# A two-lane decoder on one core: part of the second self attention's preparation moves from VectorE to GpSimd and ScalarE, with a new hand-written order

## The chip, the cores and the metric

The kernel is one launch on one core of a Trainium2 chip. The metric is device time in microseconds (us). The engines are TensorE (PE, matmuls; PEld is its weight load), VectorE (DVE), ScalarE (ACT), GpSimd (POOL) and SyncE (SP, which issues the DMAs). Each runs its own instruction stream in order and waits for others only by semaphores.

## The reference, cut to what matters

Two decoder layers on `x` of shape 4 x 256 x 128, six stages one after another, each added to `x`:

```python
x = x + _L0_attn_ref(_layernorm(x), ...)          # l0a: self attention, 16 heads, relative bias
x = x + _L0_xattn_ref(_layernorm(x), ctx, ctx)    # l0x: cross attention, 16 heads of 64
x = x + _L0_ffn_ref(_layernorm(x), ...)           # ffn: quantized, depthwise convolution, silu
x = x + _L1_attn_ref(_layernorm(x), ...)          # l1a: self attention (below)
x = x + _L1_xattn_ref(_layernorm(x), ctx, ctx)    # l1x: attention over heads within a token
x = x + _L1_ffn_ref(_layernorm(x), ...)           # moe: 8 experts, top 2, and a shared one
```

The stage that the change edits:

```python
def _L1_attn_ref(x, Wq, Wk, Wv, Wp, bp):          # H = 16, DQ = 4, HEAD_OUT = 8, keys and values shared by tiling
    q = x @ Wq
    k = jnp.tile(x @ Wk, (1, 1, G))
    v = jnp.tile(x @ Wv, (1, 1, G))
    ...
    scores = jnp.einsum('bhqd,bhkd->bhqk', q, k)
    scores = jnp.where(causal, -jnp.inf, scores)
    scores = (scores + _alibi_bias(t, scores.dtype)) / jnp.sqrt(jnp.asarray(DQ, scores.dtype))
    w = jax.nn.softmax(scores, axis=-1)
    ctx = jnp.einsum('bhqk,bhkd->bqhd', w, v).reshape(b, t, D_OUT)
    return ctx @ Wp + bp
```

## The kernel before

The four batches are cut into two lanes, A and B, of two batches each (512 tokens, held as 4 tiles of 128 tokens). Each lane runs the six stages in turn, in its own SBUF area and its own four PSUM banks; tile names begin with the lane and the stage (`A_l1a_qT`). Both lanes share the engines, so one lane's matmuls can run while the other lane is in a stretch of short dependent steps. A lane's stage begins when that lane's `x` of the stage before is updated.

What stands in which place in an engine's stream is decided by hand-written tables. Each stage has one generator per engine (`tensor`, `vector`, `scalar`, `gpsimd`, `sync`) which yields between pieces of work. `merged` (behind `TURNS`) steps through the generators of lane A, lane B, the weight levels (W) and late loads (L) in the order that a string such as `A4 B2 A2 W1` gives: four pieces of A, two of B, and so on. The yielded numbers only order pieces within one lane and stage; the engines' streams of the two lanes are mixed by `TURNS` alone. The numbers in the table are not times.

In l1a (`alibi_attention`, L1281) a projection of a token tile lands in PSUM as 80 query and key columns and 32 value columns, in float32. The scores are taken in bfloat16 from three parts of each number, high, middle and low:

- DVE (`split`, L1459 on) rounds the 80 columns to the high part (L1466), subtracts it (L1469, the rest), rounds the rest to the middle part (L1472) and subtracts that to get the low part (L1475). The link semaphore keeps each step behind the one before.
- POOL copies the queries' parts into a stack of 32 rows per head (L1392); ACT copies the values out of PSUM (L1406) and the keys' parts into the stack (L1410).
- PE transposes the stack in five groups (L1602), four of queries and one of keys, into two banks in turn. Group g waits for the copy of group g - 2.
- DVE copies the five groups from PSUM: four copies to `qT` (L1506, 128x512 bf16) and four of 32 rows to `kT` (L1510). `kT` and `vals` are set to zero before, by DVE (L1496, L1497), and the ones column of `vals` is set by DVE too (L1487).
- POOL's first work in the stage is the normalization's `rstd` (L160), which needs the variance that DVE wrote (L156), and on which DVE's four `xn` instructions wait (L165).

Beside this, l1a computes the keys and values of the later stage l1x from the context, which is known long before: 16 products per lane (L1561, L1566), biased by DVE (L1456) and ACT (L1401). They are the matmuls that can run while the preparation runs.

The cross attention of the first layer is l0x, with 32 head units per lane (16 heads, two batches). In a unit PE makes scores (L993, L995), DVE takes the maximum (L922), ACT the exponentials (L842), POOL the scaling by the sums (L825), PE three transposes (L1007), ACT the eviction (L859), PE the value products (L1020) and DVE an eviction for two units (L936). At the end comes the output product (L1028). In ffn, the silu (L1129) needs another activation table than the exponential (L842, L379).

## Time and profile before

| | before |
|---|---|
| median of 3 runs | 604.96 us (604.09 to 607.64) |
| profiled execution, whole time | 606.53 us |
| its span, first to last instruction | 604.6 us |
| PE busy | 522.7 us (86%) |
| DVE busy | 427.1 us (71%) |
| ACT busy | 330.7 us (55%) |
| POOL busy | 191.4 us (32%) |
| mean granted PE clock | 0.950 of full speed |

Shares of the chain that ended last: PE 64%, DVE 19%, ACT 5%, issue 5%, POOL 3%, DMA 2%. A stage's place in the span is read from the first and last start of its instructions: lane A runs ffn from about 244 to 292 us and l1a from there to 420; lane B runs ffn from 300 to 335 us and l1a from there to 432. The share of an engine over the whole span says little here, since the stages load the engines differently. The stretches by windows say more.

### The profile page before, as it was taken

The numbers are of one execution on the slowest core, as the hardware profiler recorded it, in microseconds if no ns is written. First come the engines' busy times: TensorE is split into PE (matmuls) and PEld (weight loads), VectorE is DVE, ScalarE is ACT, GpSimd is POOL, SyncE is SP. The second block draws the span as 40 slices with busy tenths as digits, with TensorE's granted clock in tenths as the row PEclk, the third lists the DMA queues.
The fourth block names the chain that finished last, engine by engine and source line by source line (L and its number), as shares of the span: only waits on it lengthen the run. The fifth ranks groups of instructions, "written<-read, shape, count | busy, mean of one in ns | idle before, by whom it ended". The sixth has DMA issues, their size and how long they took to land.

```text
span 604.6 us, 13037 instructions
## 1 busy us (share of the span) xinstructions
PE 522.7 (86%) x4832; PEld 323.9 (54%) x4842; DVE 427.1 (71%) x1261; ACT 330.7 (55%) x819; POOL 191.4 (32%) x288
## 2 busy tenths in 40 slices
...
GB/s 291 285 3 3 2 2 4 1 2 1 1 140 1 1 2 2 1 2 1 1 277 128 106 129 87 36 3 4 1 1 3 3 3 1 125 16 141 0 2 35
DMA packets 25890, 27.93 MB, mean 46 GB/s; under 512 B 18250, under 2 KB 22867, under 8 KB 24931
## 3 DMA queue, kind: packets, MB, share of 16 engines
...
## 4 chain that ended last, share of the span: by engine, by line
PE 64%; DVE 19%; ACT 5%; issue 5%; POOL 3%; DMA 2%; SPq 1%; POOLq 0%; DVEq 0%; ACTq 0%; another core or an unknown queue 0%
PE A_banks L312 4%; PE B_banks L312 4%; PE A_banks L2098 3%; PE B_banks L2098 3%; PE A_banks L1020 2%; PE A_banks L1007 2%; DVE A_l0a_nmax L340 2%; PE B_banks L1007 2%; PE B_banks L1823 2%; PE B_banks L1020 2%; PE B_banks L248 1%; PE B_banks L975 1%; PE A_banks L975 1%; PE B_banks L962 1%; PE B_banks L960 1%
## 5 line engine op out<-in xcount | busy, mean ns | idle before, releaser
L825 POOL TENSOR_TENSOR B_l0x_prob<-B_l0x_prob,B_l0x_inverted_sums 128x256 f32<-128x256 f32 (+1 forms) x32 | 26.0, 834 | 43.6 <-DVE B_l0x_inverted_sums L940 43.6
L825 POOL TENSOR_TENSOR A_l0x_prob<-A_l0x_prob,A_l0x_inverted_sums 128x256 f32<-128x256 f32 (+1 forms) x32 | 25.9, 829 | 39.3 <-DVE A_l0x_inverted_sums L940 39.2
L379 ACT ACTIVATE A_l0a_expT<-A_banks 128x512 f32<-128x512 f32 x32 | 18.6, 608 | 29.5 <-PE A_banks L327 29.5
L2098 PE MATMUL A_banks<-A_moe_xT,w_moe_rows 128*128 128x512 f32 x72 | 34.5, 597 | 0.1
L2098 PE MATMUL B_banks<-B_moe_xT,w_moe_rows 128*128 128x512 f32 x72 | 34.0, 595 | 0.0
L340 DVE TENSOR_REDUCE A_l0a_nmax<-A_banks 128x2 f32<-128x512 f32 x32 | 21.8, 689 | 14.6 <-PE A_banks L248 14.1
L842 ACT ACTIVATE A_l0x_prob<-A_l0x_prob,A_l0x_nmax 128x128 f32<-128x128 f32 x64 | 28.2, 447 | 2.5 <-DVE A_l0x_nmax L922 2.5
L842 ACT ACTIVATE B_l0x_prob<-B_l0x_prob,B_l0x_nmax 128x128 f32<-128x128 f32 x64 | 28.2, 446 | 0.9 <-DVE B_l0x_nmax L922 0.9
L340 DVE TENSOR_REDUCE B_l0a_nmax<-B_banks 128x2 f32<-128x512 f32 x32 | 21.8, 687 | 9.0 <-PE B_banks L248 8.6
L160 POOL TENSOR_TENSOR A_l0a_rstd<-A_l0a_ve,w_const_rows 128x4 f32<-128x4 f32 x2 | 2.0, 1012 | 79.9 <-DVE A_l0a_ve L156 79.9
L379 ACT ACTIVATE A_l1a_expT<-A_banks 128x384 f32<-128x384 f32 x32 | 15.3, 494 | 20.1 <-PE A_banks L292 20.1
L859 ACT ACTIVATE B_l0x_probT<-B_banks 128x384 f32<-128x384 f32 x32 | 15.5, 483 | 18.6 <-PE B_banks L1007 18.6
L379 ACT ACTIVATE B_l0a_expT<-B_banks 128x512 f32<-128x512 f32 x32 | 18.5, 606 | 10.2 <-PE B_banks L327 10.2
L1994 ACT ACTIVATE B_moe_h<-B_banks,w_moe_rest_rows 128x512 f32<-128x512 f32 x18 | 12.3, 686 | 20.8 <-PE B_banks L2098 20.6
L1007 PE MATMUL B_banks<-w_const_rows,B_l0x_prob 128*128 128x128 f32 x96 | 17.7, 295 | 6.4 <-ACT B_l0x_probT L859 4.1
L1994 ACT ACTIVATE A_moe_h<-A_banks,w_moe_rest_rows 128x512 f32<-128x512 f32 x18 | 12.3, 684 | 18.5 <-PE A_banks L2098 18.5
L859 ACT ACTIVATE A_l0x_probT<-A_banks 128x384 f32<-128x384 f32 x32 | 15.5, 484 | 10.9 <-PE A_banks L1007 10.8
L922 DVE CUSTOM_DVE_ANT_0 A_l0x_prob<-A_banks,A_l0x_mask_q 128x128 f32<-128x128 f32 x64 | 18.9, 351 | 3.4 <-PE A_banks L995 3.3
L379 ACT ACTIVATE B_l1a_expT<-B_banks 128x384 f32<-128x384 f32 x32 | 15.3, 492 | 10.0 <-PE B_banks L292 9.9
L340 DVE TENSOR_REDUCE B_l1a_nmax<-B_banks 128x2 f32<-128x512 f32 (+1 forms) x24 | 16.3, 687 | 6.0 <-PE B_banks L256 5.6
L340 DVE TENSOR_REDUCE A_l1a_nmax<-A_banks 128x2 f32<-128x512 f32 (+1 forms) x24 | 16.3, 689 | 5.9 <-PE A_banks L256 5.6
L922 DVE CUSTOM_DVE_ANT_0 B_l0x_prob<-B_banks,B_l0x_mask_q 128x128 f32<-128x128 f32 x64 | 18.9, 349 | 1.4 <-PE B_banks L995 1.4
...
## 6 DMA issues: line engine op xcount, KB each, us to landing
...
```

What stands on the lines that cost most here:

```text
L312: ins = pe.matmul(bank[r:r + self.rows, second:S], lhsT, rhs, start=(part == 0), stop=(part == parts - 1), skip_group_check=True)
L340: dve.tensor_reduce(out, scores, AX, ALU.max, negate=True).then_inc(self.s_mx.sem, 1)
L379: act.activation(self.expT[:, u % self.ring, :], self.exp_bank(u)[:, 0:self.W], ACT.Exp, scale=self.scale).then_inc(self.s_p.sem, 1)
L825: ins = pool.tensor_tensor(pair, pair, bcast(rz[:, g % 2, i, :], 2, n), ALU.mult)
L842: ins = act.activation(part, part, ACT.Exp, bias=nmax[:, b, i, h:h + 1], scale=-1.0, accum_out=zsum[:, g % 2, i, u % 2:u % 2 + 1])
L859: act.activation(probT[:, u % 4, :], bank[2][:, 0:W], ACT.Copy).then_inc(s_pt.sem, 1)
L922: ins = dve.tensor_tensor_reduce(prob[:, (2 * p + j) % RING, at:at + n], bank[j][:, at:at + n], mask_q[:, b, at:at + n], 1.0, 3e38, ALU.ad ...
L975: pe.matmul(q_bank(c)[:, :], w["l0x_q"][:, c * P:(c + 1) * P], xT[:], start=True, stop=True).then_inc(s_q.sem, 1)
L1007: ins = pe.transpose(bank[2][:, c * P:(c + 1) * P], prob[:, u % RING, c * P:(c + 1) * P], w["ident"][:])
L1020: ins = pe.matmul(bank[3][HD * j:HD * (j + 1), part * P:S], vals[:, b * SB + part, h * HD:(h + 1) * HD], pT[:, S:W] if part else pT[:, 0:S ...
L1994: act.activation(h1[:, n % 2, :], hidden_bank(2 * n)[:, :], ACT.Identity, bias=w["moe_b1"][:, e, part:part + 1]).then_inc(s_h1.sem, 1)
L2098: pe.matmul(hidden_bank(k)[:, :], w["moe_w3" if which else "moe_w1"][:, ORDER[i], part, :], xT[:], start=True, stop=True).then_inc(s_h.sem, 1)
```

## The change

Four edits in l1a and one in the tables:

- The middle rounding and the low difference of the split are POOL's (2 instructions per tile, 4 tiles, per lane). DVE signals the rest (`s_rest`), POOL signals the middle part (`s_mid`) and then the low one (`s_split`).
- ACT's copy of the values waits for `s_rest` and no longer for `s_split`, and the keys' copies are a piece of their own.
- The four copies of the queries' transposed parts are ACT's. The keys' ones stay with DVE, with a semaphore of their own (`s_qT`, `s_kT` in place of `s_qkT`).
- `kT` and `vals` are zeroed by POOL at the start of its stage, and the ones column is set by POOL behind `rstd`.
- `TURNS` has new strings for all five engines, so the two lanes are mixed in another way from l0a to moe.

```diff
@@ gpsimd
+        yield 0.5
+        pool.memset(kT[:], 0.0).then_inc(s_kz.sem, 1)
+        pool.memset(vals[:], 0.0).then_inc(s_kz.sem, 1)
         yield 1.5
         w.loaded(pool, "l1a")
         norm.gpsimd_rstd(pool)
         yield 1.6
         yield 2.0
+        pool.wait_ge(*s_kz(2))
+        pool.memset(vals[:, :, :, DV:DV + 1], 1.0).then_inc(s_init.sem, 1)
...
         for t in range(TT):
-            yield 9.0 + 3.5 * t
+            yield 8.5 + 3.5 * t
+            pool.wait_ge(*s_rest(t + 1))
+            mid, lo, rest = sp_[:, t % 2, 1, :], sp_[:, t % 2, 2, :], sr[:, t % 2, :]
+            pool.tensor_copy(mid, rest).then_inc(s_mid.sem, 1)
+            yield
+            pool.wait_ge(*s_mid(t + 1))
+            pool.tensor_tensor(lo, rest, mid, ALU.subtract).then_inc(s_split.sem, 1)
+            yield
             pool.wait_ge(*s_split(t + 1))
@@ scalar, values(t)
+            act.wait_ge(*s_rest(t + 1))
+            act.activation(vals[:, t, :, 0:DV], ...).then_inc(s_v.sem, 1)
+            yield 9.5 + 3.5 * t
             act.wait_ge(*s_split(t + 1))
-            act.activation(vals[:, t, :, 0:DV], ...).then_inc(s_v.sem, 1)
...
         yield from interleaved([all_keys(), all_values()])
+        for g in range(4):
+            yield 22.0 + g
+            act.wait_ge(*s_stT(g + 1))
+            act.activation(qT[:, g, :], stack_bank(g).bitcast(BF16), ACT.Copy).then_inc(s_qT.sem, 1)
@@ vector, split
-            link.add(dve.tensor_tensor(sr[:, t % 2, :], qk, hi, ALU.subtract))
-            yield due
-            link.wait()
-            link.add(dve.tensor_copy(mid, sr[:, t % 2, :]))
-            yield due
-            link.wait()
-            dve.tensor_tensor(lo, sr[:, t % 2, :], mid, ALU.subtract).then_inc(s_split.sem, 1)
+            dve.tensor_tensor(sr[:, t % 2, :], qk, hi, ALU.subtract).then_inc(s_rest.sem, 1)
@@ vector
-        dve.memset(kT[:], 0.0).then_inc(s_kz.sem, 1)
-        dve.memset(vals[:], 0.0).then_inc(s_kz.sem, 1)
         yield from interleaved([all_values(), all_splits()])
-        for g in range(5):
...
+        yield 26.0
+        dve.wait_ge(*s_kz(2))
+        dve.wait_ge(*s_stT(5))
+        for j in range(HK):
+            r = slice(SW * j, SW * (j + 1))
+            ins = dve.tensor_copy(kT[r, j, :], stack_bank(4).bitcast(BF16)[r, :])
+        ins.then_inc(s_kT.sem, 1)
@@ TURNS (all five strings are new; the first line of one)
-        "A4 B2 A2 B2 A5 B2 A3 B3 A4 B2 A1 B3 A10 B3 A3 B1 A1 B1 ...
+        "A4 B2 A2 B2 A5 B2 A3 B3 A1 B2 A2 B1 A2 B1 A3 B1 A7 B9 ...
```

Three places of the new order follow. The first is ACT's stream around lane A's silu. L842 is the exponential of lane B's cross attention, L859 its eviction, L1136 and L1129 lane A's convolution and silu. Before:

```order
L842 ACTIVATE B_l0x_prob,B_l0x_zsum<-B_l0x_prob,B_l0x_nmax 128x256
L859 ACTIVATE B_l0x_probT<-B_banks 128x384
L1129 ACT_TABLE_LOAD
L1129 ACTIVATE A_ffn_conv<-A_ffn_conv 128x512 x4
L859 ACTIVATE B_l0x_probT<-B_banks 128x384
L842 ACT_TABLE_LOAD
L842 ACTIVATE B_l0x_prob,B_l0x_zsum<-B_l0x_prob,B_l0x_nmax 128x128
L842 ACTIVATE B_l0x_prob,B_l0x_zsum<-B_l0x_prob,B_l0x_nmax 128x256
```

Now:

```order
L859 ACTIVATE B_l0x_probT<-B_banks 128x384
L1136 ACTIVATE A_ffn_conv<-A_ffn_h,w_ffn_rows 128x512 x2
L1129 ACT_TABLE_LOAD
L1129 ACTIVATE A_ffn_conv<-A_ffn_conv 128x512 x4
L1143 ACTIVATE A_ffn_r<-A_banks,A_ffn_scale 128x512 x4
L1146 ACTIVATE A_ffn_q2T<-A_banks 128x1024
L1124 ACTIVATE B_ffn_rowinv<-B_banks 128x512
```

All of lane B's exponentials now stand ahead of lane A's silu, so the table is not loaded back for them, and it is still the right one at lane B's silu. Before, there are three loads from here to the end of lane B's silu, now there is one; the load before the exponentials of l1a (L379) stands in both.

The second place is PE's stream from lane A's sums over the hidden columns (L1253) through its transposes (L1262) and down product (L1269). L1007, L993, L995, L1020 and L1028 are lane B's cross attention. Before:

```order
L1253 MATMUL A_banks<-w_const_rows,A_ffn_conv 128x128 x16
L1007 MATMUL B_banks<-w_const_rows,B_l0x_prob 128x128 x3
L993 MATMUL B_banks<-B_l0x_kT,B_l0x_qT 128x128 x2
L995 MATMUL B_banks<-B_l0x_kT,B_l0x_qT 128x256 x2
L1007 MATMUL B_banks<-w_const_rows,B_l0x_prob 128x128 x3
L1020 MATMUL B_banks<-B_l0x_probT,B_l0x_vals 64x256 x2
L1020 MATMUL B_banks<-B_l0x_probT,B_l0x_vals 64x128 x2
```

Now (L1235 is the first product of lane B's ffn, L1563 lane A's context values):

```order
L1028 MATMUL B_banks<-w_l0x_vo_rows,B_l0x_qT 128x128 x16
L1253 MATMUL A_banks<-w_const_rows,A_ffn_conv 128x128 x16
L1262 MATMUL A_banks<-w_ident_bf,A_ffn_q_114 128x128 x16
L1269 MATMUL A_banks<-w_ffn_q,A_ffn_q2T 128x128 x16
L1235 MATMUL B_banks<-B_ffn_diag,w_const_rows 128x128 x4
L1563 MATMUL A_banks<-w_l1x_rows,A_ctxT 128x512
L1240 MATMUL B_banks<-w_ident_bf,B_ffn_xq 128x128 x4
```

Lane B's cross attention is now over, with its output product, ahead of lane A's sums. Behind lane A's own output product (its last L1028) 19 units of lane B had their transposes left before, and 9 have now. At the first row of lane B in l1a, the streams of both kernels stand at the same piece in both lanes again.

The third place is POOL's stream where lane B enters l1a. Before:

```order
L1392 COPY A_l1a_expT<-A_l1a_split 128x16x4 x2
L160 TENSOR_TENSOR B_l1a_rstd<-B_l1a_ve,w_const_rows 128x4
L1375 TENSOR_TENSOR B_l1a_row_bias<-w_l1a_rows 128x32
L1376 MEMSET B_l1a_expT 128x80x2
L1378 TENSOR_TENSOR B_l1a_row_bias<-B_l1a_row_bias,w_l1a_rows 128x32
```

Now:

```order
L1405 COPY A_l1a_expT<-A_l1a_split 128x16x4 x2
L1371 MEMSET B_l1a_kT 128x2048
L1372 MEMSET B_l1a_vals 128x512
L160 TENSOR_TENSOR B_l1a_rstd<-B_l1a_ve,w_const_rows 128x4
L1379 MEMSET B_l1a_vals 128x16
L1381 TENSOR_TENSOR B_l1a_row_bias<-w_l1a_rows 128x32
```

The two memsets stand between the start of the stage and `rstd`, and the larger has 2048 elements per partition, where DVE's had 1024 (of four bytes each).

## Rows read from the trace of the kernel before

**Rows 1.** Windows; us, busy us of each engine (x instructions), clock, DMA share, GB/s

```profile
core 0: us, PE busy (x) PEld busy (x) DVE busy (x) ACT busy (x) POOL busy (x), PEclk, DMA share, GB/s
...
244.30:345.80 101.50, 77.51 (x528) 49.45 (x529) 84.32 (x268) 58.27 (x154) 32.16 (x74) 0.90 0.25 75
345.80:604.60 258.80, 233.43 (x2626) 161.08 (x2632) 190.28 (x442) 127.82 (x244) 73.05 (x76) 0.98 0.11 35
```

**Rows 2.** The same view, lane B's ffn beside lane A's l1a

```profile
292.00:335.00 43.00, 34.12 (x219) 20.85 (x217) 36.41 (x107) 23.16 (x54) 11.59 (x37) 0.92 0.49 148
```

**Rows 3.** The chain that ended last, 333 to 341 us: start, us, what

```profile
333.91 1.13 DVE B_x L1229 x4
335.03 0.33 DVE A_l1a_qT L1506
...
337.75 0.30 DVE A_l1a_qT L1506
...
339.59 0.91 DVE B_l1a_kT L1496
...
340.56 0.48 DVE B_l1a_vals L1497
```

**Rows 4.** Instructions of one line; xcount: duration in ns min/median/max, first and last start

```profile
L1472 DVE CAST A_l1a_split<-A_l1a_rest_qk x4: 191/198/201, 307.8 to 331.9; 128x80 bf16<-128x80 f32 x4
...
L1475 DVE TENSOR_TENSOR A_l1a_split<-A_l1a_rest_qk,A_l1a_split x4: 232/234/243, 310.1 to 332.8; 128x80 bf16<-128x80 f32 x4
...
L1506 DVE COPY A_l1a_qT<-A_banks x4: 414/416/425, 334.9 to 337.7; 128x512 bf16<-128x512 bf16 x4
```

**Rows 5.** Instructions of one line, as in rows 4, for POOL

```profile
L497 POOL CAST A_l0a_split<-A_l0a_rest_qk x4: 396/400/400, 17.3 to 29.5; 128x256 bf16<-128x256 f32 x4
...
L500 POOL TENSOR_TENSOR A_l0a_split<-A_l0a_rest_qk,A_l0a_split x4: 667/668/678, 17.8 to 30.0; 128x256 bf16<-128x256 f32 x4
...
L1379 POOL MEMSET A_l1a_parts<- x1: 522/522/522, 297.1 to 297.1; 128x512 bf16 x1
```

**Rows 6.** Instructions of one line, for an ACT copy of 512 columns

```profile
L1423 ACT ACTIVATE A_l1a_xT<-A_banks x1: 598/598/598, 303.8 to 303.8; 128x512 f32<-128x512 f32 x1
```

**Rows 7.** Timeline: start, us, engine, line, instruction, idle before it and its releaser

```profile
336.93 1.01 POOL L160 TENSOR_TENSOR B_l1a_rstd<-B_l1a_ve,w_const_rows 128x4 f32<-128x4 f32 x1 [2.97 <-DVE B_l1a_ve L156]
```

**Rows 8.** Timeline of ACT around lane A's silu, 272 to 278 us

```profile
272.27 1.28 ACT L1129 ACT_TABLE_LOAD   x1
...
273.57 2.19 ACT L1129 ACTIVATE A_ffn_conv<-A_ffn_conv 128x512 f32<-128x512 f32 x4
...
276.15 1.28 ACT L842 ACT_TABLE_LOAD   x1
```

**Rows 9.** Groups, 244.3 to 345.8 us: xcount | busy us, mean ns | idle before, releaser

```profile
L859 ACT ACTIVATE B_l0x_probT<-B_banks 128x384 f32<-128x384 f32 x19 | 9.2, 483 | 12.6 <-PE B_banks L1007 12.6
...
L922 DVE CUSTOM_DVE_ANT_0 B_l0x_prob<-B_banks,B_l0x_mask_q 128x128 f32<-128x128 f32 (+1 forms) x28 | 8.3, 349 | 0.5 <-PE B_banks L995 0.5
...
L936 DVE COPY B_l0x_qT<-B_banks 128x256 f32<-128x256 f32 x11 | 4.6, 420 | 4.7 <-PE B_banks L1020 4.7
...
L922 DVE DVE_READ_ACCUMULATOR2_ANT B_l0x_nmax<- 128x1 f32 x28 | 2.2, 80 | 0.0
...
L940 DVE RECIPROCAL B_l0x_inverted_sums<-B_l0x_zsum 128x4 f32<-128x4 f32 x8 | 1.4, 172 | 0.8 <-ACT B_l0x_prob L842 0.7
```

**Rows 10.** Groups of PE, 190 to 240 us, lane B's units

```profile
L1007 PE MATMUL B_banks<-w_const_rows,B_l0x_prob 128*128 128x128 f32 x39 | 6.9, 285 | 1.0 <-DVE B_l0x_qT L875 0.9
...
L995 PE MATMUL B_banks<-B_l0x_kT,B_l0x_qT 64*128 64x256 f32 x30 | 4.6, 377 | 0.0
L1020 PE MATMUL B_banks<-B_l0x_probT,B_l0x_vals 128*64 128x256 f32 (+1 forms) x40 | 4.3, 336 | 0.0
L993 PE MATMUL B_banks<-B_l0x_kT,B_l0x_qT 64*128 64x128 f32 x32 | 3.9, 322 | 0.0
```

**Rows 11.** Instructions of one line: lane A's xn in l1a, 128x128

```profile
L165 DVE TENSOR_SCALAR A_l1a_xn<-A_x,A_l1a_mv,A_l1a_rstd x4: 327/530/882, 296.6 to 297.7; 128x128 f32<-128x128 f32 x4
```

More of the change, by code:

```diff
@@ L1404, in values @@
         def values(t):
+            act.wait_ge(*s_rest(t + 1))
+            act.activation(vals[:, t, :, 0:DV], bank[2 + t % 2][:, NQK:W].rearrange("p (h d) -> p h d", h=HK), ACT.Copy).then_inc(s_v.sem, 1)
+            yield 9.5 + 3.5 * t
             act.wait_ge(*s_split(t + 1))
-            act.activation(vals[:, t, :, 0:DV], bank[2 + t % 2][:, NQK:W].rearrange("p (h d) -> p h d", h=HK), ACT.Copy).then_inc(s_v.sem, 1)
             for part, i, n in split_columns(K_PARTS):
@@ L1427, in all_values @@
                     act.wait_ge(*s_init(2))
-                values(t)
+                yield from values(t)
         yield from interleaved([all_keys(), all_values()])
+        for g in range(4):
+            yield 22.0 + g
+            act.wait_ge(*s_stT(g + 1))
+            act.activation(qT[:, g, :], stack_bank(g).bitcast(BF16), ACT.Copy).then_inc(s_qT.sem, 1)
         for n in range(U + 8):
@@ L1464, in split @@
             qk = bank[2 + t % 2][:, 0:NQK]
-            hi, mid, lo = (sp_[:, t % 2, i, :] for i in range(3))
+            hi = sp_[:, t % 2, 0, :]
             link.add(dve.tensor_copy(hi, qk))
@@ L1484, in all_splits @@
         def all_splits():
-            yield 3.0
-            dve.wait_ge(*s_kz(2))
-            dve.memset(vals[:, :, :, DV:DV + 1], 1.0).then_inc(s_init.sem, 1)
             for t in range(TT):
```

27 lines of the change are left out of this document (9 added, 18 removed), and 46 rows, old and new, of the table TURNS.

## The prediction

> **What bounds the kernel now.** I read the windows first, since a share over the whole span mixes six stages in two lanes. I cut the span at two events: the end of lane A's output product of the cross attention, at 244.3 us, and lane A's first masked score product, at 345.8 us. Between them lie both feed-forward stages and the preparation that the change edits. There PE is busy 77.5 of 101.5 us at a mean clock of 0.90, while DVE is busy 84.3 us; behind 345.8 us PE is busy 233.4 of 258.8 us at 0.98 [rows 1]. So most of PE's idle time to be had by this change lies in the middle stretch, and DVE is the busiest engine in it. With lane B's feed-forward beside lane A's preparation DVE has 36.4 of 43.0 us, a share of 0.847 [rows 2]. The chain of waits was read next, for what of the edited work lies on the path. It goes through DVE with three copies of the queries' parts of lane A and then both memsets of lane B [rows 3]. PE, and everything of lane B behind it, waits there.
>
> **The edit, DVE's side.** Per lane go 4 middle roundings of 0.198 us, 4 low differences of 0.234 us and 4 copies of 0.416 us [rows 4], which is 3.39 us, and memsets of 0.91 and 0.48 us [rows 3], together 4.8 us; the ones memset is too small to count. In the middle stretch this is all of lane A's and the memsets of lane B, 4.8 + 1.4 = 6.2 us. On the chain itself I find 0.91 + 0.48 for lane B's memsets and about 1.0 us for three copies, of which the first and the last stand with 0.33 and 0.30 us [rows 3], so 2.4 us. That is the least that leaves; the most is the whole of 6.2 us.
>
> **The edit, what it adds.** POOL gets a middle rounding and a low difference per tile. The same pair in the first self attention takes 0.396 and 0.668 us at 256 columns [rows 5]; at 80 columns I bound it by those from above and by 80/256 of them from below (0.12 and 0.21), and take 0.26 and 0.35. Behind them on POOL stand the queries' stack copies and behind these PE's transposes. Only the last tile of a lane can be late by it, by some 0.3 us, and in lane A that is covered by lane B's tail. The keys' parts on ACT wait as long, but the values no longer wait for the low part. ACT's copies of the queries' parts: a copy of 512 float32 columns takes 0.598 us there [rows 6] against 0.416 on DVE, so 0.18 us more for each of four. The groups alternate between two banks and no longer queue behind lane B's statistics on DVE, so I take nothing for lane A; without that cover it is 0.7 us per lane.
>
> The memsets in front of `rstd` are a real price. POOL's memset of 512 bf16 elements takes 0.522 us [rows 5]. At that rate 2048 elements take 2.1 us; the least is DVE's 0.91 us [rows 3]. With `vals`, 0.5 us, POOL is busy 2.6 us from the start of the stage. In lane B the stage starts at 335.04 us, when `x` is done [rows 3], and `rstd` starts at 336.93 us [rows 7], 1.9 us later. So `rstd` is late by 0.7 us (nothing if the memset is as quick as DVE's), and with it `xn`, on which the chain stands. Lane A has feed-forward work of lane B to do on DVE meanwhile. I take +0.7 us.
>
> **The new order.** It changes three things that I can price.
>
> First, two table loads go. Lane A's silu stays behind its load at 272.27 us; the reload for lane B's exponentials, 1.28 us at 276.15 us [rows 8], goes, and so does the load of lane B's silu, which is off the chain. Between 0 and 2.6 us; it is part of the stretch below and is not counted twice. ACT starts its first silu at 273.57 us, at once behind the load that took 1.28 us from 272.27 us [rows 8]. The Trainium skill (ScalarE: Activation LUTs, section What ACT_TABLE_LOAD costs) says that a switch costs a drain of about 1.38 us besides its 1.283 us. The load agrees with the row, and the drain does not show in it; by the page two switches would be worth 5.3 us, by the row 2.6 us.
>
> Second, lane B is further on when lane A leaves the cross attention. 19 of its evictions stood in the middle stretch [rows 9], and 9 stand there now by the order. So 10 units move ahead. Their work on PE per unit, from lane B's groups between 190 and 240 us, is 6.9/13 + 4.6/15 + 4.3/10 + 3.9/16 = 1.51 us [rows 10] (the counts divided by 3, 2, 4 and 2 instructions per unit). PE is the bound ahead of the cut, so the first stretch grows by 10 x 1.51 = 15.1 us. Their work on DVE is 8.3/14 + 2.2/14 + 4.6/22 + 1.4/16 = 1.05 us per unit [rows 9] (two L922 and two accumulator reads per unit, one L936 and one L940 per two units).
>
> Third, with 10 units and the edit gone, DVE has 84.3 - 6.2 - 10.5 = 67.6 us of work in the middle stretch. At the share of 0.847 [rows 2] it takes 67.6 / 0.847 = 79.8 us. If DVE never paused it would take 67.6 us, and at the share of the stretch before, 84.3 / 101.5 [rows 1], 81.4 us. I take 79.8, since rows 2 is already the mixture of lane B's feed-forward with lane A's preparation that the new stretch mostly is. So the middle shrinks by 101.5 - 79.8 = 21.7 us, and 15.1 us of that is given back ahead of it: 6.6 us remain.
>
> Against this stands that PE now has nothing of lane B between lane A's hidden sums and its down product. PE's clock in the stretch is 0.90 already [rows 1], and a further pause may drop it to the lower of its two levels (1.2 of 2.4 GHz) for the matmuls that follow. I take +1 us, between 0 and 5. Behind the second cut both orders stand at the same piece when lane B enters the second self attention, and the work behind it is the same; I take 0, within 3 us either way, for an order of which no row shows the effect.
>
> **Sum.** -6.6 + 0.7 + 1.0 = -4.9 us. On the profiled execution (606.53 us, its span 604.6 us) this gives 601.6 us. The median of the runs is 604.96 us, 1.6 us below it, so the forecast is 604.96 - 4.9 = 600.0 us, rounded.
>
> **The rivals.**
>
> *POOL's new work holds DVE up.* The four xn instructions of lane A, of one shape, took 0.327 us at the quickest and 0.882 at the slowest [rows 11], and POOL was busy then. If each of lane A's and lane B's 8 new instructions stops DVE for its own length, this costs 8 x (0.26 + 0.35) = 4.9 us, and the forecast goes back to 604.9 us: no change. For it speaks the spread of rows 11; against it, that the instructions are short and DVE would have to be at one of the hindered forms each time. The Trainium skill states such a rule (SBUF — State Buffer, section Who interferes with whom): GpSimd and VectorE share one pair of ports, taken whole for an instruction, and copies, casts and tensor_scalar of VectorE can need it. The spread of rows 11 agrees.
>
> *The new mixture is worth nothing, and only the edit's part on the chain counts.* This is the case if the units moved ahead cost there what they free later. Then it is -2.4 + 0.7 = -1.7 us, 603.3 us: no change too. For it speaks that the work of every engine is the same in total; against it, that 10 units cost PE 15.1 us and the DVE-bound stretch more.
>
> *PE stands uncovered between the two feed-forward stages, and it is slower.* Lane A's chain from the hidden sums to `x` has had lane B's heads beside it, and now lane B's own feed-forward begins only at its end. If the two stages then follow each other rather than overlap, the middle stretch is twice the 35 us that lane B's stage takes (300 to 335 us) plus the 11 us from there to 345.8 us, and 9 units of 1.51 us before, 94.6 us. With 15.1 us given back ahead, 0.7 us for `rstd` and 2 us of lower clock it is 94.6 - 101.5 + 15.1 + 2.7 = +10.9 us, 615.9 us; halfway there, 608 us. It decides from a middle stretch of 84.7 us on (101.5 - 15.1 - 1.7). For it speaks the order of PE's stream; against it, that on DVE lane B's statistics already stand among lane A's last steps.
>
> **How the numbers follow.** The forecast has 0.50, of which some 0.08 is a stretch nearer to DVE never pausing (67.6 us, which would give 588 us). The port rival has 0.13, the neutral mixture 0.13, the uncovered PE 0.24. A change within 0.5% (3 us) can't be told from none, so faster is below 601.9 us and slower above 608.0 us. The forecast lies 1.9 us below the first bound, and some of its cases fall short of it (0.06), while a few of the rivals' come out faster: faster 0.48, same 0.29, slower 0.23. The range is 591 to 611 us: half of the way to an unpaused DVE on one side, and most of the way to the third rival on the other. The forecast's own range is 595 to 604 us.
>
> **What would show it.** In the profile after: the time from the end of lane A's last L1028 to its first masked score near 80 us, against 101.5; the first of these near 259 us, against 244.3; two table loads fewer; DVE's busy time in l1a less by 4.8 us per lane; POOL's memset of `kT` near 2.1 us and lane B's `rstd` 2.6 us behind its `x`; the xn and copies of DVE no slower than 0.88 us beside POOL. It would be wrong if the first cut moved by much more than 15 us, if the middle stretch stayed above 85 us, or if a difference of over 3 us arose behind the second cut.

## The result, and the profile after

The changed kernel takes 588.07 us (median of 4 runs, 586.74 to 589.35) against 604.93 us before (4 runs, 604.09 to 607.64): a ratio of 0.972, 95% interval 0.968 to 0.976, so 16.9 us faster. Forecast were 600.0 us and a range of 591 to 611. Two further sets of runs gave 588.28 us (0.971, 0.968 to 0.975) and 589.0 us (0.974, 0.970 to 0.978). The profiled execution has a span of 587.6 us, 17.0 less than the one that the prediction read.

The windows of the changed kernel, cut at the events of [rows 1] and also where lane A's l0x begins (126.0 us) and where its l1x begins (408.7 us). Columns as in [rows 1].

```profile
0.00:126.00 126.00, 100.53 (x1010) 50.72 (x1011) 85.46 (x232) 66.00 (x151) 34.21 (x69) 0.91 0.20 71
126.00:253.50 127.50, 123.05 (x816) 73.47 (x815) 81.23 (x379) 91.88 (x321) 60.33 (x79) 1.00 0.05 18
253.50:330.10 76.60, 58.45 (x386) 35.69 (x386) 66.99 (x192) 44.55 (x106) 30.97 (x78) 0.89 0.28 91
330.10:408.70 78.60, 73.81 (x891) 53.89 (x890) 52.67 (x147) 45.28 (x116) 5.88 (x24) 0.98 0.22 60
408.70:587.50 178.80, 159.96 (x1740) 108.03 (x1744) 136.81 (x284) 83.56 (x132) 71.14 (x60) 0.98 0.08 28
```

The first cut comes at 253.5 us, 9.2 later than before; the middle stretch has 76.6 us against 101.5, 24.9 less; what follows has 257.5 against 258.8, 1.3 less [rows 1]. The sum is -17.0 us. The same view of the kernel before, for the two halves of its first stretch (lane A's l0x begins at 124.9 us) and the two parts behind the middle:

```profile
0.00:124.90 124.90, 96.69 (x891) 48.40 (x892) 83.43 (x223) 60.41 (x139) 34.04 (x69) 0.88 0.20 72
124.90:244.30 119.40, 115.11 (x793) 65.00 (x793) 69.05 (x329) 84.16 (x282) 52.15 (x69) 1.00 0.05 19
345.80:421.00 75.20, 68.38 (x839) 50.20 (x838) 54.89 (x156) 40.16 (x105) 3.69 (x17) 1.00 0.20 54
421.00:604.60 183.60, 165.05 (x1790) 110.87 (x1796) 135.39 (x287) 87.66 (x139) 69.36 (x60) 0.97 0.08 27
```

Compare row by row. In the second half PE is busy 96% of the time in both kernels, and the new order's extra work there, 7.9 us of PE, costs 8.1 us. In the first half 119 more matmuls run (1010 against 891), and the stretch grows by 1.1 us only. PE had paused there for 28.2 of 124.9 us, at a mean clock of 0.88. Now it pauses for 25.5 us, at 0.91, and its busy time is only 3.8 us higher.

Lane B's head units that are left for the middle stretch, to be held against [rows 9] (19 evictions, 28 maxima, 11 copies):

```profile
L859 ACT ACTIVATE B_l0x_probT<-B_banks 128x384 f32<-128x384 f32 x9 | 4.3, 483 | 6.7 <-PE B_banks L1007 6.7
L936 DVE COPY B_l0x_qT<-B_banks 128x256 f32<-128x256 f32 x6 | 2.5, 420 | 0.5 <-PE B_banks L1020 0.4
```

The new instructions of POOL and ACT in lane B's l1a (count, ns min/median/max, starts):

```profile
L1371 POOL MEMSET B_l1a_kT<- x1: 1805/1805/1805, 322.1 to 322.1; 128x2048 bf16 x1
L1396 POOL CAST B_l1a_split<-B_l1a_rest_qk x4: 249/254/254, 334.1 to 345.8; 128x80 bf16<-128x80 f32 x4
L1399 POOL TENSOR_TENSOR B_l1a_split<-B_l1a_rest_qk,B_l1a_split x4: 336/337/338, 334.5 to 346.1; 128x80 bf16<-128x80 f32 x4
L1449 ACT ACTIVATE B_l1a_qT<-B_banks x4: 592/594/597, 349.2 to 352.4; 128x512 bf16<-128x512 bf16 x4
```

And two places of its timeline, where such a memset meets DVE (start, us, instruction, idle before it):

```profile
291.85 1.80 POOL L1371 MEMSET A_l1a_kT<- 128x2048 bf16 x1 [1.36 <-DVE A_x L1229]
292.62 1.78 DVE L1182 TENSOR_SCALAR B_ffn_r<-B_ffn_r 128x512 f32<-128x512 f32 x1
293.59 0.52 POOL L1372 MEMSET A_l1a_vals<- 128x512 f32 x1
...
322.11 1.80 POOL L1371 MEMSET B_l1a_kT<- 128x2048 bf16 x1 [0.24 <-DVE B_x L1229]
...
323.41 0.99 DVE L156 TENSOR_SCALAR B_l1a_ve<-B_l1a_mv 128x4 f32<-128x4 f32 x1
...
323.85 0.52 POOL L1372 MEMSET B_l1a_vals<- 128x512 f32 x1
...
324.55 1.02 POOL L160 TENSOR_TENSOR B_l1a_rstd<-B_l1a_ve,w_const_rows 128x4 f32<-128x4 f32 x1 [0.17 <-DVE B_l1a_ve L156]
```

Lane B's variance step takes 0.99 us (0.17 for lane A's), and the feed-forward's L1182 1.78 us (0.41 to 0.43 for lane A and in the kernel before). `rstd` starts 2.5 us behind `x`.

The forecast expected PE to pause in the middle stretch and to be slower behind it. These are the two rows of the changed kernel in which that happens (columns as in [rows 1]):

```profile
276.90:284.30 7.40, 2.44 (x19) 1.80 (x18) 6.92 (x26) 3.50 (x7) 1.11 (x3) 1.00 0.79 296
284.30:294.60 10.30, 7.78 (x42) 5.22 (x42) 9.69 (x30) 2.58 (x4) 3.74 (x6) 0.50 0.18 73
```

### The profile page after: what moved, and what is told of

The parts are those of the page before. It is cut to its first block, busy times and chain, and to the rows that moved or that the text cites. A ratio compares the mean times of both kernels' runs of the same rounds, so it can differ in the third digit from the quotient of the medians.

```text
span 587.6 us, 13037 instructions
## 1 busy us (share of the span) xinstructions
PE 515.8 (88%) x4832; PEld 321.8 (55%) x4842; DVE 423.2 (72%) x1231; ACT 331.3 (56%) x825; POOL 202.5 (34%) x310
## 4 chain that ended last, share of the span: by engine, by line
PE 65%; DVE 18%; ACT 4%; issue 4%; SPq 3%; POOL 3%; DMA 2%; POOLq 0%; DVEq 0%; ACTq 0%
PE A_banks L2101 5%; PE A_banks L312 4%; PE B_banks L312 4%; PE B_banks L2101 4%; DVE A_l0a_nmax L340 2%; PE A_banks L1007 2%; PE A_banks L1020 2%; DMA B_l1x_values<-B_l1a_v_tokens 2%; PE B_banks L1867 2%; SPq L276 1%; PE B_banks L1007 1%; DVE B_l0a_nmax L340 1%; PE B_banks L1028 1%; PE A_banks L1877 1%; SPq L1364 1%
## 5 line engine op out<-in xcount | busy, mean ns | idle before, releaser
L379 ACT ACTIVATE A_l0a_expT<-A_banks 128x512 f32<-128x512 f32 x32 | 18.3, 604 | 20.5 <-PE A_banks L327 20.5
L842 ACT ACTIVATE B_l0x_prob<-B_l0x_prob,B_l0x_nmax 128x128 f32<-128x128 f32 x64 | 28.2, 446 | 1.3 <-DVE B_l0x_nmax L922 1.3
L842 ACT ACTIVATE A_l0x_prob<-A_l0x_prob,A_l0x_nmax 128x128 f32<-128x128 f32 x64 | 28.2, 449 | 0.0
L379 ACT ACTIVATE B_l0a_expT<-B_banks 128x512 f32<-128x512 f32 x32 | 18.2, 601 | 15.0 <-PE B_banks L327 15.0
L859 ACT ACTIVATE A_l0x_probT<-A_banks 128x384 f32<-128x384 f32 x32 | 15.5, 484 | 15.6 <-PE A_banks L1007 15.6
L379 ACT ACTIVATE A_l1a_expT<-A_banks 128x384 f32<-128x384 f32 x32 | 15.1, 491 | 15.2 <-PE A_banks L292 15.0
L859 ACT ACTIVATE B_l0x_probT<-B_banks 128x384 f32<-128x384 f32 x32 | 15.4, 482 | 14.3 <-PE B_banks L1007 14.2
L379 ACT ACTIVATE B_l1a_expT<-B_banks 128x384 f32<-128x384 f32 x32 | 15.1, 493 | 11.8 <-PE B_banks L292 11.5
L1007 PE MATMUL B_banks<-w_const_rows,B_l0x_prob 128*128 128x128 f32 x96 | 17.2, 289 | 5.0 <-POOL B_l0x_prob L825 2.0
```

The costliest lines, as they stand in the source:

```text
L379: act.activation(self.expT[:, u % self.ring, :], self.exp_bank(u)[:, 0:self.W], ACT.Exp, scale=self.scale).then_inc(self.s_p.sem, 1)
L842: ins = act.activation(part, part, ACT.Exp, bias=nmax[:, b, i, h:h + 1], scale=-1.0, accum_out=zsum[:, g % 2, i, u % 2:u % 2 + 1])
L859: act.activation(probT[:, u % 4, :], bank[2][:, 0:W], ACT.Copy).then_inc(s_pt.sem, 1)
L1007: ins = pe.transpose(bank[2][:, c * P:(c + 1) * P], prob[:, u % RING, c * P:(c + 1) * P], w["ident"][:])
```

## The experiments

Ratios are to the kernel before, on the same chip, with 95% intervals. Where an order is made from two, the tables alone differ; of these the first PE line that differs is shown (A and B are the lanes, the number is how many pieces; e3 and e11 against the changed kernel, e4 and e10 against e2).

### Order or edit

**e1, e13: the order alone.** The code before, with the new tables. DVE's 24 displaced pieces of both lanes had to be placed; e1 puts them beside their neighbours, e13 by their time.

```diff
-"A4 B2 A2 B2 A5 B2 A3 B3 A4 B2 A1 B3 A10 B3 A3 B1 A1 B1 A2 B3 A1 B1 A1 B2 A1 B1 A1 B1 A1 B3 A6 B1 A2 B2 A1 B1 A3 B2 A2 B3 A3 B1 A1 B2 A1 B2 A5 B4 A3 B1 A1 "
+"A4 B2 A2 B2 A5 B2 A3 B3 A1 B2 A2 B1 A2 B1 A3 B1 A7 B9 A1 B1 A1 B3 A2 B1 A1 B2 A6 B2 A1 B3 A2 B1 A1 B5 A1 B1 A1 B1 A1 B1 A4 B1 A1 B1 A1 B2 A3 B1 A1 B1 A1 B2 "
```

> The kernel before with the changed kernel's order of pieces on every engine; the DVE instructions that the edit took away stay on DVE, right behind the piece they belong to, and lane B's copies of the queries' parts stand together. Theory 1 (the order carries most of it: the middle stretch, and in the first self attention the two lanes stand nearer in step, so that PE has more to do between 60 and 80 us and gets its full clock earlier; the edit is worth only its 4 to 5 us): 592 to 594 us, first cut near 253.5 us. Theory 2 (the edit alone makes the gain, the order is only its carrier): 604 to 606 us. Theory 3 (neither alone, they need each other, because the order was made for the lighter DVE): over 600 us here and over 600 us with the edit alone.

> As the order alone, but DVE's middle roundings, low differences and copies of the queries' parts stand in DVE's order at the time at which GpSimd and ScalarE do them in the changed kernel, one by one between the other lane's pieces. Theory 1 (the gap between the order alone and both is real, lane A's copies into kT and lane B's xn queue up on DVE): 594 to 597 us, as the first version at 596.1. Theory 2 (the gap is made by the bunched copies): 590 to 592 us.

Measured: 596.13 us, 0.9875 (0.9856 to 0.9894), and 593.03 us, 0.9813 (0.9790 to 0.9835). Both times lie nearest to the first theory of e1, e1's 2 us above its range, and e13's between its own two ranges. So the order alone is worth 11.3 us (9.9 to 12.7), two thirds of the result. The two placings of the displaced pieces are 3 us apart, so the placing matters as much as one of the edit's parts. Windows of e13: the first half, and the middle.

```profile
0.00:126.80 126.80, 101.54 (x1010) 51.05 (x1011) 85.35 (x231) 66.06 (x151) 34.30 (x69) 0.89 0.20 71
...
254.30:333.90 79.60, 58.29 (x385) 35.71 (x385) 70.70 (x210) 42.70 (x102) 23.79 (x64) 0.89 0.29 91
```

**e2, e14: the edit alone.** The changed code with the old tables, placed in the same two ways.

```diff
-"A4 B2 A2 B2 A5 B2 A3 B3 A1 B2 A2 B1 A2 B1 A3 B1 A7 B9 A1 B1 A1 B3 A2 B1 A1 B2 A6 B2 A1 B3 A2 B1 A1 B5 A1 B1 A1 B1 A1 B1 A4 B1 A1 B1 A1 B2 A3 B1 A1 B1 A1 B2 "
+"A4 B2 A2 B2 A5 B2 A3 B3 A4 B2 A1 B3 A10 B3 A3 B1 A1 B1 A2 B3 A1 B1 A1 B2 A1 B1 A1 B1 A1 B3 A6 B1 A2 B2 A1 B1 A3 B2 A2 B3 A3 B1 A1 B2 A1 B2 A5 B4 A3 B1 A1 "
```

> The changed kernel's code with the order of pieces of the kernel before (the new pieces of GpSimd and ScalarE stand where they come ready; one score product of lane A goes ahead of lane B's third group of stack transposes, without which the order locks). Theory 1: the edit is worth 4 to 5 us by what it takes off the chain in the second self attention, so 600 to 601 us, with the first cut unchanged at 244 us. Theory 2: 588 us. Theory 3: over 600 us, at or above the kernel before.

> As the edit alone, but GpSimd's and ScalarE's new pieces stand where their DVE forms began in the kernel before, and no product of lane A is moved ahead. Theory 1 (in the old order lane B's statistics and PE's queue, not the edited work, set lane B's time, so the edit brings nothing): 603 to 605 us. Theory 2 (the edit's gain was lost by the placing of ScalarE's copies): 599 to 601 us.

Measured: 604.64 us, 0.9997 (0.9978 to 1.0016), and 602.2 us, 0.9980 (0.9957 to 1.0003). e2 misses the 600 to 601 us of its first theory, and e14 lies between its two. In the old order the edit is worth 1.2 us, or nothing. In the new one it is worth the step from 0.9813 to 0.971 to 0.974, 4 to 6 us with some 3 us of uncertainty. The windows of e14 and e2 show where it would have come:

```profile
245.10:342.60 97.50, 74.61 (x529) 46.69 (x529) 78.94 (x250) 60.32 (x158) 38.93 (x88) 0.93 0.27 76
```

```profile
0.00:121.40 121.40, 95.04 (x891) 48.52 (x892) 82.71 (x222) 60.44 (x139) 34.51 (x69) 0.90 0.21 74
...
240.90:338.10 97.20, 74.09 (x527) 47.96 (x527) 79.44 (x250) 60.33 (x158) 38.75 (x88) 0.93 0.25 75
338.10:599.20 261.10, 233.95 (x2626) 161.36 (x2632) 187.13 (x430) 130.22 (x248) 75.44 (x84) 0.98 0.11 36
```

DVE pauses for 18.6 us in e14's middle, and for 17.2 in the kernel before [rows 1]; with the new order it is 8.9 us in e13 and 9.6 in the changed kernel. That less work on DVE buys little where it pauses anyway fits these figures, but no run tests it by itself.

**e9: the kernel before, profiled again.**

> The kernel before, profiled a second time, to see how much of a stretch's length is the clock of one execution. Theory 1 (the profiled execution that the prediction read had 30.7 us at the lower clock before its first cut, where the kernel with the edit alone, whose work is the same up to there, had 23.9 us and came to the cut at 240.6 us against 244.0): with 24 us at the lower clock the first cut is at 241 us here and the middle stretch 98 to 102 us. Theory 2 (the clock plays no part, the 3.4 us are the edit's): cut at 244 us whatever the clock.

```profile
0.00:127.50 127.50, 99.52 (x891) 50.23 (x892) 84.02 (x223) 60.53 (x139) 34.03 (x69) 0.85 0.19 70
127.50:246.90 119.40, 115.13 (x793) 65.00 (x793) 69.06 (x329) 84.15 (x282) 52.15 (x69) 1.00 0.05 19
246.90:347.10 100.20, 77.22 (x529) 49.10 (x529) 84.05 (x268) 58.32 (x154) 32.16 (x74) 0.90 0.25 76
```

The clock came out lower, not higher, so the expectation's case didn't occur. Its rule holds: with the same 891 matmuls in the first half, clocks of 0.85, 0.88 and 0.90 (e9, before, e2) go with 127.5, 124.9 and 121.4 us. One profile of the first half is good to 3 us, no better, so all of them are averaged here. The six with the old order have 121.4 to 127.5 us, 124.9 on average, and the thirteen with the new order 125.0 to 127.9, 126.4 on average: 1.5 us more. The second half has 119.4 or 119.5 us in every profile with the old order throughout, and 127.4 or 127.5 with the new one. The first cut comes at 244.3 us on average with the old order (four profiles) and at 253.8 us with the new one (twelve), 9.5 us later.

### Where the order's gain comes from

**e3: new order in the first half, old behind.**

```diff
-"A1 B1 A1 B1 A1 B1 A2 B3 A1 B1 A2 B1 A2 B1 A1 B1 A3 B1 A1 B1 A3 B1 A4 B1 A1 B1 A3 B1 A8 B4 A1 B2 A1 B1 A1 B2 A1 B2 A1 B1 A2 B2 A1 B1 A1 B1 A2 B1 A1 B3 A4 B1 "
+"A1 B1 A1 B1 A1 B1 A2 B3 A1 B1 A2 B1 A2 B1 A1 B1 A3 B1 A1 B1 A3 B1 A4 B1 A1 B1 A3 B1 A15 B4 A1 B1 A2 B1 A1 B1 A2 B1 A2 B1 A1 B1 A2 B1 A3 B1 A2 B1 A3 B1 A2 "
```

> The changed kernel's code; the new order up to the start of lane A's cross attention (about 124 us), the old order for all that is left. Theory 1: the first self attention keeps its better clock, and lane A leaves it no later than before although lane B is further on; behind it the old order has fewer pieces of lane B left to place. 595 to 599 us. Theory 1b (the first stage's order brings nothing, all comes behind 124 us): 601 to 606 us, since lane B's lead made there is bought with lane A's time and given away by the old order.

602.77 us, 0.9987 (0.9965 to 1.0009). The first half has 127.3 us, within the range of the new order; the second 115.1 us, 4.3 less than before, but the middle is 98.7 us. The first stage's order brings nothing by itself (theory 1b): the old order spends lane B's lead before the middle.

**e4: old order in the first half, new behind. e10: old order up to lane A's ffn, new behind.** The new order expects lane B further on; the missing pieces of B then run in one go, 19 on PE in e4, 32 in e10:

```diff
-"B2 A2 B2 A4 B1 A1 B1 A4 B2 A1 B2 A1 B1 A2 B3 A1 B1 A1 B2 A1 B4 A2 B1 A1 B7 A1 B1 A2 B1 A1 B1 A2 B1 A2 B1 A1 B1 A2 B1 A3 B1 A2 B1 A3 B1 A2 B1 A2 B1 A1 B1 A1 "
+"B2 A2 B2 A4 B1 A1 B1 A1 B19 A6 B4 A1 B2 A1 B1 A1 B2 A1 B2 A1 B1 A2 B2 A1 B1 A1 B1 A2 B1 A1 B3 A4 B1 A2 B2 A3 B2 A2 B1 A3 B2 A1 B1 A4 B4 A2 B1 A1 B2 A2 B1 "
...
-"B12 A2 B3 A1 B7 A1 B8 A1 B1 A1 B1 A2 B2 A1 B7 A11 B3 A4 B1 A5 B4 A1 B1 A8 B1 A12 B4 A2 B2 A2 B1 A2 B4 A2 B1 A2 B3 A3 B1 A2 B1 A1 B7 A2 B4 A1 B4 A1 B4 A1 B2 "
+"B32 A2 B1 A1 B8 A6 B1 A1 B1 A1 B1 A9 B1 A7 B4 A1 B1 A10 B2 A12 B3 A2 B2 A2 B1 A2 B4 A2 B1 A2 B3 A2 B1 A1 B3 A1 B1 A2 B16 A1 B4 A4 B3 A2 B1 A1 B2 A6 B2 A1 "
```

> The changed kernel's code; the old order up to the start of lane A's cross attention, the new order behind it. Theory 1: PE's clock before 100 us is as in the kernel before (23 us at its lower level without a break, and again at 77 and 84 us), and the rest is as in the changed kernel: 588 + 4 to 6 = 592 to 594 us. Theory 1b: 588 us, as the changed kernel, within 0.5%.

> The changed kernel's code; the old order up to lane A's first piece of the feed-forward stage, the new order behind it: lane B's 10 units that the new order has ahead of this point now stand behind it, all before lane A's feed-forward. Theory 1 (the 10 units cost PE their 13 us wherever they stand without cover, and what counts is that DVE has only 9 left beside the feed-forward stages): lane A's feed-forward begins 11 to 13 us behind the first cut of 241 to 244 us, then as the changed kernel: 588 to 591 us. Theory 2 (it counts that they lie beside lane A's heads, where they fill PE's pauses): 594 to 600 us.

598.89 us, 0.9913 (0.9884 to 0.9943), and 601.35 us, 0.9944 (0.9914 to 0.9974). Both miss theory 1, e4 also its theory 1b, and e10 lies 1.4 us above the range of its theory 2: built this way, lane B's lead costs most of what it is worth. Windows of e4 (the first half as before, the catching up, both of these together, from there to the first cut, the middle):

```profile
0.00:124.90 124.90, 96.77 (x886) 49.30 (x890) 83.41 (x222) 60.44 (x139) 34.06 (x69) 0.88 0.20 72
124.90:141.40 16.50, 12.77 (x114) 5.71 (x106) 2.57 (x11) 8.43 (x17) 0.00 (x0) 1.00 0.00 0
0.00:141.40 141.40, 109.54 (x992) 55.00 (x992) 85.98 (x232) 68.88 (x156) 34.06 (x69) 0.89 0.18 63
141.40:267.40 126.00, 120.79 (x833) 72.50 (x834) 81.18 (x379) 88.69 (x315) 60.34 (x79) 0.99 0.05 18
267.40:341.80 74.40, 56.99 (x386) 34.90 (x387) 66.37 (x192) 44.50 (x106) 31.27 (x78) 0.91 0.29 94
```

And e10's catching up, and its time from there to the second cut:

```profile
244.20:268.10 23.90, 18.86 (x156) 12.72 (x154) 13.02 (x58) 13.78 (x51) 8.16 (x10) 1.00 0.00 1
268.10:340.60 72.50, 54.92 (x372) 33.68 (x374) 65.92 (x193) 43.99 (x105) 31.41 (x78) 0.91 0.29 95
```

Not all of e4's 16.5 us is the price of catching up. Of the 114 matmuls 12 are lane A's products of the context, 5.9 us, which lane A needs anyway:

```profile
L962 PE MATMUL A_banks<-A_ctxT,w_l0x_rows 128*128 128x512 f32 x8 | 3.9, 605 | 0.0
L960 PE MATMUL A_banks<-w_l0x_vo_rows,A_ctxT 128*128 128x512 f32 x4 | 2.0, 619 | 0.0
```

The fair comparison is the time at which lane A can begin its feed-forward. e4 has run the same matmuls by then as the changed kernel, e10 12 more, and they get there at 267.4 us (e4), 268.1 (e10) and 253.5 (changed). Against the 244.3 us before, the lead costs 23 or 24 us where lane A stands still for it, and 9 us where it is mixed in. Of the 13.9 us between e4 and the changed kernel 7.2 are pauses of PE (37.1 against 29.9) and 6.7 are its busy time (230.3 against 223.6), for the same work. The busy time can be less by the clock (0.89 and 0.99 in e4's two windows, 0.91 and 1.00 in the changed kernel's) and by matmuls that follow more closely on each other; no run separates the two.

**e11: new order up to lane B's l1a, old behind.**

```diff
-"A1 B1 A1 B1 A2 B1 A2 B1 A3 B1 A1 B1 A1 B12 A2 B1 A1 B8 A6 B1 A1 B1 A1 B1 A9 B1 A7 B4 A1 B1 A10 B2 A12 B3 A2 B2 A2 B1 A2 B4 A2 B1 A2 B3 A2 B1 A1 B3 A1 B1 A2 "
+"A1 B1 A1 B1 A2 B1 A2 B1 A3 B1 A1 B1 A1 B12 A2 B1 A1 B8 A6 B1 A1 B1 A1 B1 A9 B1 A7 B4 A1 B1 A10 B1 A12 B4 A2 B2 A2 B1 A2 B4 A2 B1 A2 B3 A3 B1 A2 B1 A1 B7 A2 "
```

> The changed kernel's code; the new order up to lane B's second self attention (322 us), the old order behind it. Theory 1 (as predicted, the order behind that point is worth nothing, within 3 us): 587 to 591 us. Theory 2 (in the profiles the changed kernel needs 178.9 us from lane A's last cross attention to its end against 183.6 us, 4.7 us less, and the three kernels with the new order there all need 178 to 179 us): 591 to 594 us.

591.46 us, 0.9785 (0.9747 to 0.9824), 3 us above the changed kernel, with overlapping intervals and at the border between the two theories. In the profile the part behind the second cut has 260.4 us against 257.4, of which lane A's l1x and what follows is 181.9 against 178.8 us:

```profile
328.70:407.20 78.50, 69.81 (x840) 51.27 (x838) 52.26 (x145) 42.61 (x110) 6.17 (x25) 0.98 0.23 61
407.20:589.10 181.90, 163.52 (x1789) 110.36 (x1794) 135.22 (x287) 87.59 (x139) 69.33 (x60) 0.98 0.08 28
```

### The parts of the edit, in the new order

**e5** and **e17** are the changed kernel again.

> The changed kernel, timed once more beside its variants, so that each is compared on the same chip. 588 us, 587 to 590. Theory 1 (of the gap of 8 us between the order alone, 596.1 us, and both, all is real): the same ratio to the kernel before as in the first comparison, 0.972. Theory 2 (part of that gap is the difference between two sets of runs): 0.975 to 0.98.

> The changed kernel beside e16: 587 to 589 us, ratio to the kernel before 0.971 to 0.974.

Their figures stand at the head of this part. **e6, e7, e8** each give DVE one part back:

```diff
 # e6
-            pool.tensor_copy(mid, rest).then_inc(s_mid.sem, 1)
+            dve.tensor_copy(mid, rest).then_inc(s_mid.sem, 1)
...
-            pool.tensor_tensor(lo, rest, mid, ALU.subtract).then_inc(s_split.sem, 1)
+            dve.tensor_tensor(lo, rest, mid, ALU.subtract).then_inc(s_split.sem, 1)
 # e7
-            act.activation(qT[:, g, :], stack_bank(g).bitcast(BF16), ACT.Copy).then_inc(s_qT.sem, 1)
+            dve.tensor_copy(qT[:, g, :], stack_bank(g).bitcast(BF16)).then_inc(s_qT.sem, 1)
 # e8
-        pool.memset(kT[:], 0.0).then_inc(s_kz.sem, 1)
-        pool.memset(vals[:], 0.0).then_inc(s_kz.sem, 1)
+        dve.memset(kT[:], 0.0).then_inc(s_kz.sem, 1)
+        dve.memset(vals[:], 0.0).then_inc(s_kz.sem, 1)
```

> The changed kernel with the middle rounding and the low difference of the second self attention on DVE again, 16 instructions in pieces of their own, put into DVE's order at the time at which GpSimd had them. Theory 1 (the edit is worth DVE's time in the DVE-bound middle stretch): 8 x 0.198 + 8 x 0.234 = 3.5 us slower, less what GpSimd's slower pair (0.25 + 0.34 us) gave, so 2 to 3.5 us: 590 to 591.5 us. Theory 2 (only what stands on the chain counts, and these don't): within 1 us of the changed kernel.

> The changed kernel with the four copies of the queries' transposed parts of each lane on DVE again (0.416 us each against 0.6 us on ScalarE), put into DVE's order at the time at which ScalarE had them. Theory 1 (DVE's time in the middle stretch): 4 x 0.416 = 1.7 us slower for lane A's, and lane B's stand on the chain where either engine is waited for: 588 + 1 to 2.5 us. Theory 2 (copies on the chain are quicker on DVE): 0 to 1 us faster than the changed kernel.

> The changed kernel with the two memsets of each lane on DVE again, behind its xn; the ones stay with GpSimd. Theory 1: 2 x (0.91 + 0.48) = 2.8 us more on DVE in or at the end of the middle stretch, less the 0.6 us by which rstd is earlier: 2 us slower, 590 us. Theory 2 (the sets hide behind the wait for PE's first products): within 1 us.

Measured 589.15, 589.90 and 589.67 us, beside 588.28: +0.9, +1.6 and +1.4 us, ratios 0.9748, 0.9761 and 0.9753 with intervals of 0.003 either way. None is told from nothing alone, so these runs don't decide between the theories of any of the three. Together they make 3.9 us by the medians and 7 by the ratios (each against 0.9714), which agrees with the 4 to 6 us of the whole edit. No part makes it by itself.

**e15: two table loads put back.**

```diff
         act.activation(rowinv[:], bank[0][:, :], ACT.Copy).then_inc(s_ri.sem, 1)
+        if lane.name == "B":
+            act.activation(y[:, HC - 1, 0:1], w["ident"][:, 0:1], ACT.Exp)
```

> The changed kernel with one exponential of a single column put on ScalarE between the silus of the two lanes (in lane B's feed-forward stage, behind its row copy), which costs a load for it and another for lane B's silu: two table loads of 1.28 us more, as many as in the kernel before. Theory 1 (both stand on lane B's path, which sets when its second self attention starts): 588 + 2.6 = 590.6 us. Theory 2 (the chain through that stage is DVE's, ScalarE has time there): 588 to 588.5 us. By the Trainium skill (ScalarE: Activation LUTs, What ACT_TABLE_LOAD costs) a drain of about 1.38 us would come with each load; if it does and both are on the path, 593.3 us.

587.71 us, 0.9713 (0.9682 to 0.9745), against the 0.9714 of the changed kernel: nothing, theory 2. ACT's timeline there:

```profile
291.84 0.60 ACT L1124 ACTIVATE B_ffn_rowinv<-B_banks 128x512 f32<-128x512 f32 x1 [3.86 <-PE B_banks L1237]
292.45 1.28 ACT L1126 ACT_TABLE_LOAD   x1
293.75 0.20 ACT L1126 ACTIVATE B_ffn_conv<-w_const_rows 128x1 f32<-128x1 f32 x1
...
303.69 1.28 ACT L1131 ACT_TABLE_LOAD   x1
```

The load starts 0.01 us behind the copy's end, and the exponential 0.02 us behind the load's: no drain is seen here either.

**e12, e16: the memsets elsewhere on POOL**, behind `rstd` (e12) or behind the small copies (e16), the keys' as 1024 uint32.

```diff
-        pool.memset(kT[:], 0.0).then_inc(s_kz.sem, 1)
-        pool.memset(vals[:], 0.0).then_inc(s_kz.sem, 1)
...
         norm.gpsimd_rstd(pool)
+        pool.memset(vals[:], 0.0).then_inc(s_kz.sem, 1)
+        pool.memset(kT[:].bitcast(U32), 0).then_inc(s_kz.sem, 1)
```

> The changed kernel with GpSimd's two memsets of the second self attention behind its rstd, and that of the keys as 1024 uint32 elements instead of 2048 bf16. Theory 1: rstd of lane B starts 0.6 us earlier (1.9 us behind its x, as before the change), and this stands on the chain: 587.3 to 587.7 us, a gain of 0.6 us, which 5 rounds can hardly tell. The memset of 1024 uint32 takes 0.9 us if the time goes by elements, 1.8 us if by bytes. Theory 2 (the later sets delay the values' copies on ScalarE): 588.5 us or more.

> The changed kernel with GpSimd's memsets of the second self attention (values, then keys as 1024 uint32, then the ones) behind its small copies, 2.3 us after rstd, when xn is done. Theory 1 (the memsets hold DVE's tensor_scalar instructions up): lane B's variance step takes 0.17 us and its xn 1.1 to 1.3 us, rstd starts 1.7 us behind x, and of that 0.8 to 1.4 us reach the end: 586.8 to 587.4 us if the changed kernel is at 588.2. Theory 2 (lane B's preparation waits for PE anyway): no difference that 5 rounds can tell.

589.71 us, 0.976 (0.9723 to 0.9798), and 589.34 us, 0.9754 (0.9728 to 0.978), beside e17's 589.0. By their times both miss theory 1 and agree with theory 2; what theory 1 says of the place itself happens in part. The first two rows are e12's, the other two e16's:

```profile
L1375 POOL MEMSET B_l1a_kT<- x1: 953/953/953, 326.4 to 326.4; 128x1024 uint32 x1
L165 DVE TENSOR_SCALAR B_l1a_xn<-B_x,B_l1a_mv,B_l1a_rstd x4: 336/900/1412, 326.0 to 327.8; 128x128 f32<-128x128 f32 x4
```

```profile
L156 DVE TENSOR_SCALAR B_l1a_ve<-B_l1a_mv x1: 170/170/170, 322.9 to 322.9; 128x4 f32<-128x4 f32 x1
L165 DVE TENSOR_SCALAR B_l1a_xn<-B_x,B_l1a_mv,B_l1a_rstd x4: 329/534/886, 324.3 to 325.4; 128x128 f32<-128x128 f32 x4
```

In both `rstd` starts 1.7 us behind `x`, 0.8 earlier than in the changed kernel. In e12 an xn instruction then takes up to 1.41 us (0.75 at most in the changed kernel), and the gain is gone. In e16 the variance step is not held up, and an xn takes up to 0.89 us. From the start of lane B's l1a to its first score product it has 31.1 us (321.6 to 352.7) against 31.5 (322.1 to 353.6), which no comparison of these runs can tell. No version here is faster than the changed kernel by more than the noise.

## Why the prediction was wrong

The direction and the mechanism were right: lane B further on, DVE relieved in the middle, and the middle shrinks by more than is given back ahead of it. The size was off by 12 us, in these terms. (The forecast also named 588 us, for a DVE that never pauses and a middle of 67.6 us. That this number came out is luck: the middle has 76.6 us, with 9.6 us of pauses.)

1. **Failed: "PE is the bound ahead of the cut, so the first stretch grows by 10 x 1.51 = 15.1 us."** It grew by 9.2 us. The step took one rate for the whole first stretch, from rows of 190 to 240 us [rows 10], where PE is nearly always busy. In the second half PE is the bound as the step says: +8.1 us. But to have lane B's heads earlier, its l0a has to be earlier too, and that work went into the first half, where PE was idle 23% of the time: +1.1 us for 119 matmuls. It isn't the clock of one profile: over all profiles the first half grows by 1.5 us and the cut moves by 9.5. Nor was there less work than forecast: 142 more matmuls run ahead of the cut (1826 against 1684), which are the 10 units of 11 matmuls and 32 of lane B's output product. The step left these 32 out, 3.8 us of PE in e10. PE's busy time rose by 11.8 us for them and its pauses fell by 2.6. In e4 and e10, where lane A waits meanwhile, the like costs 23 and 24 us. So what failed is the price of a matmul taken as fixed; how much of the saving is clock and how much closer matmuls stays open.
2. **Middle stretch 79.8 us, measured 76.6.** DVE's work was hit, 67.6 forecast and 66.99 measured, though as two errors that cancel: e13 has 13.6 us less DVE work by the order (10.5 forecast), and the edit takes 3.7 to 5.4 us there (6.2 forecast). The share is 0.875, not 0.847: pauses of 9.6 us, not 12.2. The changed kernel's other two profiles have 76.1 and 75.9 us.
3. **+0.7 us for `rstd` and +1.0 us for the clock.** The delay of `rstd` happened (2.5 us from `x` against 1.9), and it is inside the 76.6 us. The clock's fall happened in its place: PE is busy 2.44 of 7.40 us and then runs for 10.30 us at a granted clock of 0.50, the lower of its two levels. But over the whole middle the mean clock is 0.89 against 0.90 in a stretch that is shorter by 24.9 us, so the time at the lower level fell, by these means from about 20 to about 17 us. Adding both terms to a stretch that was sized by a share of another stretch counted them on top: 1.7 us.
4. **Behind the second cut 0, within 3 us.** It was -1.3 us. e11 puts the order's part at about 3 us, at the bound, with overlapping intervals. What the edit does there isn't settled: 261.1 us in e2 and 257.6 in e14, against 258.8 and, in e9, 257.8 for the kernel before.

5.9 + 3.2 + 1.7 + 1.3 = 12.1 us, the distance between -4.9 and -17.0.

The smaller steps: POOL's pair took 0.25 and 0.34 us (0.26 and 0.35 forecast), its memset 1.80 (2.1), ACT's copies 0.594 (0.598). DVE's total should have fallen by 9.6 us; between e13 and the changed kernel it fell by 5.6, and 2.2 of the missing 4 us are the two instructions held up by memsets. The table loads, 0 to 2.6 us, are worth 0. Of the rivals, the port rival named the right mechanism at other instructions: the delays that the rows show stand beside the memsets, none of its 4.9 us is seen as time lost to the short roundings (e6 takes them off POOL and is not faster), and e12 and e16, which move the memsets, gain nothing that these runs can tell. By the Trainium skill (SBUF — State Buffer, Who interferes with whom) when a VectorE instruction in a two-port mode meets one of GpSimd, the one that issues first has the shared ports for its whole instruction and the other blocks. The 1.78 us of L1182, which ends 0.29 us behind the second memset, agree; which mode it ran in no row shows. The neutral mixture didn't occur in the changed kernel, where the order alone gives 11.3 us, but e3, e4 and e10 come near it. The uncovered PE didn't occur: the changed kernel's middle is 8 us below the 84.7 from which the latter decides.

The forecast also took edit and order as a sum, and they are probably none. The edit gives 1.2 us in the old order and 4 to 6 in the new one, each uncertain by 1 to 3 us. A likely reason, not tested alone, is that only the new order leaves DVE few pauses.
